# Order of the column maxima's parts on four engines in the cross-attention stage of a decoder layer

## The chip, the core and the metric

The kernel runs on one core of one Trainium2 chip. The metric is the device time of one execution in microseconds (us), the median of several runs. The engines are named as the profile names them: PE is the matrix engine (PEld its weight loads), DVE the vector engine, ACT the scalar engine, POOL the gpsimd engine and SP the engine that only issues DMAs here (its queue is SPq). Each engine runs its own instructions in program order and waits for semaphores that others raise.

## The reference, cut to what matters

One decoder layer on x of 16 items x 128 rows x 512 columns: attention, cross attention and a feed-forward network with rounded weights, each added to x. The change lies in the cross stage:

```
x = x + _L0_xattn_ref(_layernorm(x), ctx_2048, w_in, b_in, w_out, b_out, w_ct, b_ct, 64)

def _L0_xattn_ref(mask, encodings, ...):      # N=16 items, E=128, T=512, H=8 heads, d=16
    qkv = transpose(mask) @ w_in.T + b_in
    scores = einsum('bqhd,bkhd->bhqk', q, k) / sqrt(d)
    band = abs(idx[:, None] - idx[None, :]) <= local_size        # 64
    scores = where(band, scores, neg)
    attn = softmax(scores)
    o = einsum('bhqk,bkhd->bqhd', attn, v) @ w_out.T + b_out
    y = relu(transpose(o)) * encodings
    return einsum('nit,io->not', y, w_ct) + b_ct[None, :, None]
```

The feed-forward network that follows rounds its weights to -1, 0 and 1 after dividing by their mean size.

## The kernel before

The kernel has three stages, one after the other: attention, the cross stage (from about 627 to 1021 us of the profile) and the feed-forward stage. The cross stage is one function, `cross`. It is a hand-written pipeline over the 16 items: `steps` runs `step(b)` for b from -3 to 18 on each engine, and each step has eight slots (s = 0 to 7) of a pair of heads and half of the tiles each. Within a step PE works on three items: in each slot it computes scores of item b+1 for their maxima (`maximum_scores` into Sm), and scores of item b with the maxima already taken off (`shifted_scores` into Se); in slots 0 to 2 it also multiplies the exponentials of item b-1 with the values (`values`), and in later slots it projects item b+3.

**The maxima.** DVE reduces Sm into `mx` (L1292), and PE may write Sm of slot s only when `mx` of slot s-1 has been read. After four slots, half an item, PE turns the maxima (`maxima_turned`, L1054 and L1055, into bank Bb). They are then split into three bf16 parts: ACT copies the high part (`maxima_high`, L1136, tile x_m), DVE takes the remainder (`maxima_rest`, L1299, x_mr), POOL makes the middle and the low part (`maxima_low`, L1191 and L1193), and SP writes the three parts as three extra rows of the tile Q of that item (`maxima_rows`, L1249, three DMAs of 4 KB). With rows of ones in K beside them, `shifted_scores` subtracts the maxima inside the matmul. It waits for these rows (m_in) in slot 0 (half 0, slots 0 to 3) and slot 4 (half 1). Half 1 of item b is turned in slot 0 of step b, and is needed in slot 4 of the same step. Half 0 of item b+1 is turned in slot 4 of step b and needed in slot 0 of step b+1.

**The queue of SP.** q and k of an item are also kept as three bf16 parts (x_qp, x_kp): `keep` writes them to DRAM (q_parts, k_parts, 384 KB each) and `spread` reads them back in the layout that the matmuls want (tiles Q and K, 768 KB each, in three and four DMAs). `spread` waits until what `keep` wrote has landed. SP also loads the context of an item (x_ctxb, 256 KB, read by POOL in L1213) and one of the 12 pieces of the feed-forward weights (`load_piece`, L58 and L60, x_w_stage, up to 768 KB). Piece n is loaded at the end of step n-1; in slot 1 of step n DVE scales and rounds it (`offset`, L1316), ahead of the maxima of slot 2; ACT writes it out in slot 2 (L1181).

In a step of before, SP's order is: context of item b-2, spread q of b+2, keep k of b+2, rows of half 1 of b, spread k of b+2, rows of half 0 of b+1, keep q of b+3, piece b+1. The order of the other engines is in the code of `step`.

## Time and profile before

| | |
|---|---|
| median of 3 runs | 1240.86 us (1239.91 to 1244.84) |
| the profiled execution | 1235.82 us, its span 1234.0 us |
| PE, DVE busy, share of the span | 84%, 66% |
| ACT, POOL busy | 52%, 52% |
| TensorE clock granted, mean of the span | 0.945 of full speed |

The profile is one execution. Its page gives busy times and the costliest groups of instructions. Other views of the same execution are used below: a table of stretches of time, a list of who waited for whom, the instructions in order of time (the timeline; a bracket at the end of a row is the idle time of the engine just before the instruction, and what ended it), and the DMAs with their times from issue to landing. The times of a row count from the start of the span.

### The profile page before, as it was taken

The numbers are of one execution on the slowest core, as the hardware profiler recorded it, in microseconds if no ns is written. First come the engines' busy times: TensorE is split into PE (matmuls) and PEld (weight loads), VectorE is DVE, ScalarE is ACT, GpSimd is POOL, SyncE is SP. The second block draws the span as 40 slices with busy tenths as digits, with TensorE's granted clock in tenths as the row PEclk, the third lists the DMA queues.
The fourth block names the chain that finished last, engine by engine and source line by source line (L and its number), as shares of the span: only waits on it lengthen the run. The fifth ranks groups of instructions, "written<-read, shape, count | busy, mean of one in ns | idle before, by whom it ended". The sixth has DMA issues, their size and how long they took to land. (4 is left out here: it accounts for less than half of the span.)

```text
span 1234.0 us, 25423 instructions
## 1 busy us (share of the span) xinstructions
PE 1035.4 (84%) x9604; PEld 774.9 (63%) x9604; DVE 813.1 (66%) x1487; ACT 647.5 (52%) x1188; POOL 640.5 (52%) x584
## 2 busy tenths in 40 slices
PE   5689999999999999999635888989899954777675
PEld 5578887888888888887413666656566631333332
DVE  7678776666666666576334667676666645888884
ACT  5555545455454545556512566666556542455553
POOL 3665666566565657566315143434334334566653
PEclk9899999999999999999867899999999976899998
DMA  9043643233233332346336666665755200000000
GB/s 348 21 172 122 246 166 120 110 138 136 81 131 133 136 113 97 133 160 211 134 75 153 149 168 164 168 160 135 187 130 135 60 19 32 18 17 25 25 25 27
DMA packets 51135, 147.57 MB, mean 120 GB/s; under 512 B 10448, under 2 KB 24272, under 8 KB 39760
## 3 DMA queue, kind: packets, MB, share of 16 engines
q1 hardware_dynamic: 42288, 86.93, 25.3%
q0 software_dynamic: 8064, 58.72, 13.0%
q8 instruction: 75, 1.23, 0.4%
q10 hardware_dynamic: 672, 0.40, 0.1%
q14 instruction: 36, 0.29, 0.1%
HBM read 120.46 MB, written 25.17 MB: 118 GB/s over the span
## 5 line engine op out<-in xcount | busy, mean ns | idle before, releaser
L1292 DVE TENSOR_REDUCE mx<-Sm 128x4 f32<-128x768 f32 x128 | 122.4, 956 | 87.7 <-PE Sm L1032 87.2
L1130 ACT ACTIVATE x_ex<-Se 128x768 f32<-128x768 f32 x128 | 103.1, 805 | 116.4 <-PE Se L1032 116.0
L282 PE MATMUL Qb<-a_xTh,WqH 128*128 128x256 f32 x512 | 146.3, 286 | 3.1 <-DVE a_vl L800 3.0
L283 PE MATMUL Qb<-a_xTl,WqH 128*128 128x256 f32 x512 | 145.6, 284 | 0.0
L284 PE MATMUL Qb<-a_xTh,WqL 128*128 128x256 f32 x512 | 145.4, 284 | 0.0
L627 POOL TENSOR_TENSOR a_pr<-a_pr_plain,a_ph 128x512 fp32r<-128x512 f32 x64 | 83.6, 1307 | 110.2 <-ACT a_ph L447 110.0
L740 DVE TENSOR_TENSOR a_turned<-Qb,sinS 64x512 f32<-64x512 f32 (+1 forms) x144 | 94.9, 659 | 62.6 <-PE Qb L284 45.1
L609 POOL TENSOR_TENSOR a_ql<-a_rot,a_qh 128x512 fp32r<-128x512 f32 x64 | 83.9, 1315 | 98.4 <-ACT a_qh L467 98.2
L459 ACT ACTIVATE Lb<-Lb 128x512 f32<-128x512 f32 x64 | 37.2, 582 | 170.4 <-PE Ob L354 170.4
L367 PE MATMUL Yb<-a_WoH,a_oH 128*128 128x512 f32 x256 | 103.2, 403 | 5.5 <-POOL a_oN L605 5.5
L282 PEld LDWEIGHTS Qb<-a_xTh,WqH 128*128 128x128 f32 x512 | 98.6, 193 | 6.9 <-issue 2.4
L369 PE MATMUL Yb<-a_WoH,a_oN 128*128 128x512 f32 x256 | 101.3, 396 | 0.0
L368 PE MATMUL Yb<-a_WoL,a_oH 128*128 128x512 f32 x256 | 101.1, 395 | 0.0
L283 PEld LDWEIGHTS Qb<-a_xTl,WqH 128*128 128x128 f32 x512 | 98.6, 193 | 2.4
L284 PEld LDWEIGHTS Qb<-a_xTh,WqL 128*128 128x128 f32 x512 | 98.6, 193 | 0.0
L605 POOL TENSOR_TENSOR a_oN<-a_oN_plain,a_oH 128x512 fp32r<-128x512 f32 x64 | 84.9, 1327 | 3.0 <-ACT a_oH L439 3.0
L1024 PE MATMUL Sm<-band,ident_b 128*64 128x256 bf16 x512 | 54.9, 296 | 31.2 <-DVE mx L1292 18.2
L756 DVE TRANSPOSE_TENSOR_REDUCE a_rmax<-Sb 128x16 f32<-128x512 f32 x64 | 45.6, 712 | 51.6 <-PE Sb L334 51.5
L1024 PEld LDWEIGHTS Sm<-band,ident_b 128*64 128x64 bf16 x512 | 19.0, 111 | 90.3 <-issue 46.1
L636 POOL TENSOR_TENSOR Dg<-ident,a_negm 32x512 fp32r<-32x512 f32 x64 | 66.5, 1039 | 13.2 <-DVE a_negm L763 10.5
L1578 POOL TENSOR_TENSOR f_hg<-f_h,g 128x512 f32<-128x512 f32 (+1 forms) x48 | 56.0, 1181 | 32.3 <-DVE f_h L1658 32.3
L1482 PE MATMUL Gb<-gateQ,f_xqT 128*128 128x512 bf16 (+1 forms) x192 | 48.0, 374 | 29.1 <-DVE f_h L1658 27.4
(202 smaller groups left out, 2841.4 us busy)
## 6 DMA issues: line engine op xcount, KB each, us to landing
a_WoH<-wo_parts POOLq DMA_DIRECT2D x28, 1024.0 KB, 5.2
a_WoL<-wo_parts POOLq DMA_DIRECT2D x28, 1024.0 KB, 7.2
K<-k_parts SPq DMA_DIRECT2D x32, 256.0 KB, 4.8
q_parts<-x_qp SPq DMA_DIRECT2D x16, 384.0 KB, 3.0
Q<-q_parts SPq DMA_DIRECT2D x16, 384.0 KB, 5.6
k_parts<-x_kp SPq DMA_DIRECT2D x16, 384.0 KB, 7.4
a_w_stage<-in_gateT SPq DMA_DIRECT2D x8, 704.0 KB, 4.5
x_w_stage<-in_gateT SPq DMA_DIRECT2D x8, 704.0 KB, 5.1
```

What stands on the lines that cost most here:

```text
L282: pe.matmul(out, w_hi(k), xTh[:, k, :], start=(k == 0), stop=False)
L283: pe.matmul(out, w_hi(k), xTl[:, k, :], start=False, stop=False)
L284: mm = pe.matmul(out, w_lo(k), xTh[:, k, :], start=False, stop=(k == KD - 1))
L367: pe.matmul(Yb[s % 2][:, :], high, WoH[u % 2][:, i, :], start=(i == 0), stop=False)
L368: pe.matmul(Yb[s % 2][:, :], high, WoL[u % 2][:, i, :], start=False, stop=False)
L369: mm = pe.matmul(Yb[s % 2][:, :], low, WoH[u % 2][:, i, :], start=False, stop=(i == HG - 1))
L605: pool.tensor_tensor(oL[:, s % 2, :], oN[:, s % 2, :], oH[:, s % 2, :].bitcast(F32), ALU.subtract).then_inc(oL_ready, 1)
L609: pool.tensor_tensor(rot_dst(False, True, par, r), rbuf(par, r)[:, 0:rot_width(r)], rot_dst(True, False, par, r).bitcast(F32), ALU.subtrac ...
L627: pool.tensor_tensor(pl[:, :], pr[:, :], ph[:, :].bitcast(F32), ALU.subtract).then_inc(pl_ready, 1)
L740: dve.tensor_tensor(dst[to:to + hi - lo, 0:width].rearrange("p (j c) -> p j c", c=P), bank[lo:hi, 0:width].rearrange("p (j c) -> p j c", c=P),
L1130: act.activation(ex[:, (PAIRS * b + p) % RING, 4 * hf * WIN:4 * (hf + 1) * WIN].rearrange("p (j c) -> p j c", j=2), Se[:, :, 0:2 * WIN], A ...
L1292: dve.tensor_reduce(mx[:, half, at:at + 4].rearrange("p (j a) -> p j a", j=2), Sm[:, :, 0:2 * WIN].rearrange("p j (a c) -> p j a c", a=2), ...
```

## The change

No instruction is added or removed in the cross stage; several stand in another place of their engine's program. For half 1 of item b, the high part moves on ACT from slot 1 to slot 0 (ahead of the exponentials of slot 0), the remainder on DVE from slot 1 to slot 0 (ahead of the update of X), the low parts on POOL ahead of the low part of k, and the rows on SP to the front of the step. For half 0 of item b+1, high part and remainder move from slot 5 to slot 4. On SP keep k now stands ahead of spread q, and the load of the context moves from the front of the next step to the end of this one, ahead of the weight piece; it loads the same item into the same place.

```
--- before.py
+++ after.py
@@ -1146,7 +1146,7 @@
 
             def step(b):
                 for s in range(SLOTS):
-                    if s == 1 and real(b):
+                    if s == 0 and real(b):
                         maxima_high(b, 1)
                     if s == 3 and real(b - 1):
                         wait(act, pv_full, b)
@@ -1156,7 +1156,7 @@
                         wait(act, out_full, b - 1)
                         wait(act, wct_full, b - 2)
                         act.activation(gate[:, :], Bb[:, :], ACT.Relu, bias=t["bo"][:, 0:1]).then_inc(gate_ready, 1)
-                    if s == 5 and real(b + 1):
+                    if s == 4 and real(b + 1):
                         maxima_high(b + 1, 0)
                     if s == 6 and real(b + 3):
                         high(qp, 0, b + 3, q_full, q_kept, q_high)
@@ -1197,6 +1197,8 @@
                 pool.tensor_tensor(dst[:, 2, :], rest[:, :], dst[:, 1, :], ALU.subtract).then_inc(ready, 1)
 
             def step(b):
+                if real(b):
+                    maxima_low(b, 1)
                 if real(b + 2):
                     low(kp, kr, b + 2, k_mid, k_low)
                 if b == -1:
@@ -1205,8 +1207,6 @@
                         wait(pool, k_ones, i)
                         pool.memset(K[i][ROWS:SHIFTED, :, :], 1.0).then_inc(k_ones, 1)
                     wait(pool, k_ones, len(K))
-                if real(b):
-                    maxima_low(b, 1)
                 if real(b - 2):
                     wait(pool, gate_ready, b - 1)
                     wait(pool, ctx_in, 16 * (b - 1))
@@ -1249,20 +1249,19 @@
                     sp.dma_start(to, m3[half][:, k, :]).then_inc(m_in[half], 16)
 
             def step(b):
-                if real(b - 2):
-                    wait(sp, y_ready, b - 2)
-                    sp.dma_start(ctxb[:, :], dram["ctx"][b - 2]).then_inc(ctx_in, 16)
-                if real(b + 2):
-                    spread("q", Q, Q_RUNS, b + 2, q_kept, q_in)
-                    keep("k", kp, b + 2, k_low, k_in, K_IN, k_kept)
                 if real(b):
                     maxima_rows(b, 1)
                 if real(b + 2):
+                    keep("k", kp, b + 2, k_low, k_in, K_IN, k_kept)
+                    spread("q", Q, Q_RUNS, b + 2, q_kept, q_in)
                     spread("k", K, K_RUNS, b + 2, k_kept, k_in)
                 if real(b + 1):
                     maxima_rows(b + 1, 0)
                 if real(b + 3):
                     keep("q", qp, b + 3, q_low, q_in, Q_IN, q_kept)
+                if real(b - 1):
+                    wait(sp, y_ready, b - 1)
+                    sp.dma_start(ctxb[:, :], dram["ctx"][b - 1]).then_inc(ctx_in, 16)
                 if 0 <= b + 1 < len(PIECES):
                     wait(sp, w_whole, b)
                     load_piece(sp, dram, b + 1, w_stage[(b + 1) % 2]).then_inc(w_in[(b + 1) % 2], 16)
@@ -1334,12 +1333,12 @@
                     if real(b + 1):
                         maxima(b + 1, s)
                     if s == 0:
+                        if real(b):
+                            maxima_rest(b, 1)
                         if real(b - 3):
                             wait(dve, wct_full, b - 2)
                             dve.scalar_tensor_tensor(out=t["X"][:, b - 3, :], in0=Ab[:, :], scalar=t["bct"][:, 0:1], in1=t["X"][:, b - 3, :],
                                                      op0=ALU.add, op1=ALU.add).then_inc(x_new, 1)
-                    if s == 1 and real(b):
-                        maxima_rest(b, 1)
                     if s == 3 and real(b - 1):
                         wait(dve, o_ready, b)
                         wait(dve, oU_scaled, b - 1)
@@ -1347,12 +1346,12 @@
                             ins = dve.stream_shuffle(rl[:, hh, :], oU[:, hh, :], [XD * (1 - hh) + i % XD for i in range(32)])
                         ins.then_inc(sums_ready, 1)
                     if s == 4 and real(b + 1):
+                        maxima_rest(b + 1, 0)
                         if real(b + 3):
                             normalised(b + 3)
                         head_values(b + 1, 0)
                     if s == 5 and real(b + 1):
                         head_values(b + 1, 1)
-                        maxima_rest(b + 1, 0)
                     if s == 6 and real(b + 3):
                         rest(qp, qr, 0, b + 3, q_high, q_low, q_rest)
                     if s == 7 and real(b + 3):
```

The queue of SP in a step with a weight piece, from the rows of half 0 to spread k of the next step. Names in the rows: x_m the parts of the maxima, x_qp and x_kp the parts of q and k in SBUF, q_parts and k_parts the same in DRAM, x_w_stage the weight piece, x_ctxb the context. Before:

```order
L1249 DMA Q<-x_m 1x32x64 [waits x_m_low]
L1249 DMA Q<-x_m 1x32x64 x2
L1234 DMA q_parts<-x_qp 128x3x512 [waits x_q_low,x_q_in]
L58 DMA x_w_stage<-in_gateT 128x1408 [waits x_w_whole]
L1254 DMA x_ctxb<-in_ctx 128x512 [waits x_y_ready]
L1241 DMA Q<-q_parts 48x4096 [waits x_se_full,x_q_kept]
L1241 DMA Q<-q_parts 32x4096
L1241 DMA Q<-q_parts 16x4096
L1234 DMA k_parts<-x_kp 128x3x512 [waits x_k_low,x_k_in]
L1249 DMA Q<-x_m 1x32x64 [waits x_m_low]
L1249 DMA Q<-x_m 1x32x64 x2
L1241 DMA K<-k_parts 16x4096 [waits x_se_full,x_k_kept]
```

The same place now:

```order
L1249 DMA Q<-x_m 1x32x64 [waits x_m_low]
L1249 DMA Q<-x_m 1x32x64 x2
L1234 DMA q_parts<-x_qp 128x3x512 [waits x_q_low,x_q_in]
L1264 DMA x_ctxb<-in_ctx 128x512 [waits x_y_ready]
L58 DMA x_w_stage<-in_gateT 128x1408 [waits x_w_whole]
L1249 DMA Q<-x_m 1x32x64 [waits x_m_low]
L1249 DMA Q<-x_m 1x32x64 x2
L1234 DMA k_parts<-x_kp 128x3x512 [waits x_k_low,x_k_in]
L1241 DMA Q<-q_parts 48x4096 [waits x_se_full,x_q_kept]
L1241 DMA Q<-q_parts 32x4096
L1241 DMA Q<-q_parts 16x4096
L1241 DMA K<-k_parts 16x4096 [waits x_se_full,x_k_kept]
```

The second group of rows of the maxima moved from behind spread q and keep k to just behind the weight piece, keep k moved ahead of spread q, and the context ahead of the piece.

On ACT, from the end of one step to slot 2 of the next, before:

```order
L1145 ACTIVATE x_qp<-x_qr 128x512 [waits x_q_rest]
L1130 ACTIVATE x_ex<-Se 128x768 [waits x_se_full] x2
L1145 ACTIVATE x_kp<-x_kr 128x512 [waits x_k_rest]
L1136 ACTIVATE x_m<-Bb 32x64 [waits x_m_in1,x_t_full]
L1130 ACTIVATE x_ex<-Se 128x768 [waits x_se_full] x2
```

The same place now:

```order
L1145 ACTIVATE x_qp<-x_qr 128x512 [waits x_q_rest]
L1130 ACTIVATE x_ex<-Se 128x768 [waits x_se_full]
L1136 ACTIVATE x_m<-Bb 32x64 [waits x_m_in1,x_t_full]
L1130 ACTIVATE x_ex<-Se 128x768 [waits x_se_full]
L1145 ACTIVATE x_kp<-x_kr 128x512 [waits x_k_rest]
L1130 ACTIVATE x_ex<-Se 128x768 [waits x_se_full] x2
```

The high part (L1136) moved from behind the exponentials of slot 0 and the middle part of k to ahead of both.

## Rows read from the trace of the kernel before

**Rows 1.** Table of stretches, two steps: PE, PEld, DVE, ACT, POOL busy, PEclk, DMA.
```profile
827.13:847.00 19.87, 18.68 (x348) 12.96 (x345) 14.85 (x25) 13.40 (x20) 8.36 (x9) 1.00 0.66 164
847.00:872.37 25.37, 20.76 (x347) 13.66 (x345) 14.63 (x25) 13.98 (x21) 8.36 (x9) 0.93 0.64 157
```

**Rows 2.** Who waited for whom, PE, 676 to 976 us: total us, times, longest.
```profile
PE Sm L1024 <- DVE mx L1292: 12.1, 8, 3.5
PE Se L1024 <- DMA Q<-x_m: 10.2, 10, 2.1
```

**Rows 3.** Timeline of PE around slots 4 and 5: start us, duration us.
```profile
811.08 0.41 PE L1024 MATMUL Se<-band,ident_b 128*64 128x256 bf16 x4 [0.18 <-ACT x_ex L1130]
...
830.09 0.41 PE L1024 MATMUL Se<-band,ident_b 128*64 128x256 bf16 x4 [0.81 <-DMA Q<-x_m]
...
831.71 0.41 PE L1024 MATMUL Se<-band,ident_b 128*64 128x256 bf16 x4 [0.38 <-ACT x_ex L1130]
```

**Rows 4.** Timeline of all engines, one step: how the rows of half 1 come about.
```profile
817.71 0.39 SPq L1234 DMA_DIRECT2D q_parts<-x_qp  x1
817.99 0.96 DVE L1292 TENSOR_REDUCE mx<-Sm 128x4 f32<-128x768 f32 x1 [0.61 <-PE Sm L1032]
818.01 0.28 PE L1055 MATMUL Bb<-ident,mx 128*32 128x64 f32 x2
818.14 0.49 SPq L58 DMA_DIRECT2D x_w_stage<-in_gateT  x1
818.67 0.59 SPq L1254 DMA_DIRECT2D x_ctxb<-in_ctx  x1
...
820.20 0.20 ACT L1136 ACTIVATE x_m<-Bb 32x64 bf16<-32x64 f32 x1
...
821.52 0.20 DVE L1299 TENSOR_TENSOR x_mr<-Bb,x_m 32x64 f32<-32x64 f32 x1
...
822.19 0.30 POOL L1193 TENSOR_TENSOR x_m<-x_mr,x_m 32x64 bf16<-32x64 f32 x1
...
823.46 1.80 SPq L1249 DMA_DIRECT2D Q<-x_m  x3
```

**Rows 5.** L1316, all twelve (ns min/median/max, first and last start); timelines, pieces 6 and 7.
```profile
L1316 DVE TENSOR_SCALAR x_w_stage<-x_w_stage,w_inv x12: 753/953/1020, 678.4 to 910.7; 128x1408 f32<-128x1408 f32 x8, 128x1536 f32<-128x1536 f32 x3, 128x1024 f32<-128x1024 f32 x1
...
804.29 0.95 DVE L1316 TENSOR_SCALAR x_w_stage<-x_w_stage,w_inv 128x1408 f32<-128x1408 f32 x1 [3.66 <-DMA x_w_stage<-in_gateT]
...
806.16 0.41 PE L1024 MATMUL Sm<-band,ident_b 128*64 128x256 bf16 x4 [2.06 <-DVE mx L1292]
...
822.73 0.95 DVE L1316 TENSOR_SCALAR x_w_stage<-x_w_stage,w_inv 128x1408 f32<-128x1408 f32 x1 [1.01 <-DMA x_w_stage<-in_gateT]
...
825.96 0.41 PE L1024 MATMUL Sm<-band,ident_b 128*64 128x256 bf16 x4
```

**Rows 6.** DMAs, us to landing: piece 7, keep q, piece 9; last, all of L1249.
```profile
x_w_stage<-in_gateT SPq DMA_DIRECT2D x1, 704.0 KB, 4.6
...
q_parts<-x_qp SPq DMA_DIRECT2D x1, 384.0 KB, 2.9
...
x_w_stage<-in_downT SPq DMA_DIRECT2D x1, 768.0 KB, 7.8
...
DMA to landing us min/median/max: 1.6/2.5/7.2
```

**Rows 7.** The start of the cross stage, timelines of SP, POOL and PE.
```profile
636.98 1.33 POOL L1197 TENSOR_TENSOR x_kp<-x_kr,x_kp 128x512 bf16<-128x512 f32 x1
...
640.90 0.42 SPq L1234 DMA_DIRECT2D k_parts<-x_kp  x1
...
646.97 1.69 SPq L1241 DMA_DIRECT2D K<-k_parts  x4
...
653.34 0.64 PE L1024 MATMUL Sm<-band,ident_b 128*64 128x256 bf16 x4 [12.76 <-DMA K<-k_parts]
```

**Rows 8.** DMA busy tenths, 636 to 654 us in 40 slices of 0.45 us.
```profile
DMA  0000699000989949499599500086999699939950
```

More of the change, by code:

```diff
@@ L1148, in step @@
                 for s in range(SLOTS):
-                    if s == 1 and real(b):
+                    if s == 0 and real(b):
                         maxima_high(b, 1)
@@ L1158, in step @@
                         act.activation(gate[:, :], Bb[:, :], ACT.Relu, bias=t["bo"][:, 0:1]).then_inc(gate_ready, 1)
-                    if s == 5 and real(b + 1):
+                    if s == 4 and real(b + 1):
                         maxima_high(b + 1, 0)
@@ L1199, in step @@
             def step(b):
+                if real(b):
+                    maxima_low(b, 1)
                 if real(b + 2):
@@ L1207, in step @@
                     wait(pool, k_ones, len(K))
-                if real(b):
-                    maxima_low(b, 1)
                 if real(b - 2):
@@ L1251, in step @@
             def step(b):
-                if real(b - 2):
-                    wait(sp, y_ready, b - 2)
-                    sp.dma_start(ctxb[:, :], dram["ctx"][b - 2]).then_inc(ctx_in, 16)
-                if real(b + 2):
-                    spread("q", Q, Q_RUNS, b + 2, q_kept, q_in)
-                    keep("k", kp, b + 2, k_low, k_in, K_IN, k_kept)
                 if real(b):
@@ L1260, in step @@
                 if real(b + 2):
+                    keep("k", kp, b + 2, k_low, k_in, K_IN, k_kept)
+                    spread("q", Q, Q_RUNS, b + 2, q_kept, q_in)
                     spread("k", K, K_RUNS, b + 2, k_kept, k_in)
@@ L1265, in step @@
                     keep("q", qp, b + 3, q_low, q_in, Q_IN, q_kept)
+                if real(b - 1):
+                    wait(sp, y_ready, b - 1)
+                    sp.dma_start(ctxb[:, :], dram["ctx"][b - 1]).then_inc(ctx_in, 16)
                 if 0 <= b + 1 < len(PIECES):
@@ L1336, in step @@
                     if s == 0:
+                        if real(b):
+                            maxima_rest(b, 1)
                         if real(b - 3):
@@ L1340, in step @@
                                                      op0=ALU.add, op1=ALU.add).then_inc(x_new, 1)
-                    if s == 1 and real(b):
-                        maxima_rest(b, 1)
                     if s == 3 and real(b - 1):
@@ L1349, in step @@
                     if s == 4 and real(b + 1):
+                        maxima_rest(b + 1, 0)
                         if real(b + 3):
@@ L1354, in step @@
                         head_values(b + 1, 1)
-                        maxima_rest(b + 1, 0)
                     if s == 6 and real(b + 3):
```

## The prediction

> **What bounds the kernel now.** I read the stage first in the table of stretches. Cut at the projection to v in slot 3 (L1105), a step takes 19 to 25 us, and PE is busy for 18.68 us of the 19.87 in a quiet one [rows 1]. DVE has 14.85, ACT 13.40, POOL 8.36. So PE is the bound of the stage, and only what makes PE wait costs time. The list of PE's waits from 676 to 976 us has two large entries that this change can touch [rows 2]. First, 10.2 us in 10 waits, up to 2.1 us each, of the shifted scores for the extra rows of the maxima (DMA Q<-x_m). In the timeline all ten stand in slot 4, where half 1 is needed [rows 3]. Second, 12.1 us in 8 waits for the maxima of DVE; six of them, 10.8 us, stand in slot 3 and follow a wait of DVE for a weight piece (pieces 0, 1, 2, 6, 9, 10: 3.5, 0.7, 0.8, 2.1, 1.5, 2.3), the other two, of 0.6, stand in the first steps.
>
> The path to the rows is in the timeline of one step [rows 4]. PE has turned the maxima by 818.29 (818.01 + 0.28). ACT copies the high part only at 820.20, DVE takes the remainder only at 821.52, POOL is done at 822.49, and SP issues the rows at 823.46, behind spread q and keep k. PE has to stop for them, from 829.28 to 830.09 [rows 3]. Hardly any of this path is work; it is places in queues.
>
> **Part 1: high part, remainder, low parts, rows to the front.** The new path, from the same rows: ACT starts at 818.3 and takes 0.20; DVE is free at 818.95 (817.99 + 0.96) and takes 0.20; POOL is through 0.77 after DVE's end (822.49 less 821.72); so the parts are ready near 819.9, and SP, through with its last issue at 819.26, sends the rows at about 820.0 instead of 823.46. That is 3.5 us earlier, and behind 704 KB of weights instead of behind weights, 768 KB of q and 384 KB of k. A row that was issued alone lands in 1.6 us, the worst took 7.2 [rows 6]. Even 7.2 gives 827.2, under the 829.28 at which PE wants them. The ten waits go: **-10.2 us**. What is late next there is ACT. The wait for the exponentials that follows each longer wait is 0.38, and where there was no wait for rows it is 0.18 [rows 3]. Eight of the ten had such a follower: 8 x 0.2 = **-1.6 us**.
>
> What the moves delay, all of it at nothing: on ACT 0.20 us ahead of the exponentials of slot 0, whose scores PE computes only after the turning that ACT waits for; on DVE 0.20 ahead of the update of X, whose reader is slots away; on POOL the low part of k, which waits for ACT's middle part, now behind the maxima's. In slot 4 DVE takes the remainder ahead of the copies of the values, in a dense stretch, with the maxima of slot 5 behind them. PE has no wait for mx in slots 4 to 7 of the full steps (the eight of [rows 2] stand in slot 3 or in the first two), so 0.2 should be hidden. If that cover is gone, it costs 0.2 x 12 = 2.4 us. On the other side ACT loses 0.1 us between the logarithm and the exponential of the sums, which releases POOL, keep q and the weight piece: each piece may start 0.1 earlier.
>
> **Part 2: the context goes ahead of the weight piece.** Before, the piece was issued at 818.14 and the context behind it [rows 4]; now 256 KB stand before it. Where each piece lands decides the maxima of slot 2 and with them PE in slot 3: piece 6 reached DVE at 804.29, and PE started slot 3 at 806.16, 1.87 later, after 2.06 of waiting. Piece 7 reached it at 822.73, so PE could have started at 824.60, and came at 825.96: 1.36 of slack [rows 5]. The same reading of the 12 executions of L1316, 678.4 to 910.7, against PE's slot 3 gives the slack of the ten pieces that have a context ahead now (2 to 11): five had none and made PE wait or just not (2, 6, 8, 9, 10), piece 5 0.04, 4 0.62, 7 1.36, 3 1.98, 11 4.9.
>
> The delay itself isn't in the trace. Keep q and piece 7 together, 1088 KB, went from the issue at 817.71 to 822.73, 5.02 us. Taking off the 1.6 of a tiny DMA [rows 6], that is 3.4 us or 320 KB per us; 256 KB are 0.8 us. Bounds: 0, if the two travel beside each other at no loss, and 1.4, if the issue of 0.59 comes on top (it should be hidden, since keep q, issued at 817.71, landed 2.9 later [rows 6]). I take 0.8, as the queue was full at that time, less the 0.1 of part 1: 0.7. Cost: pieces 2, 6, 8, 9, 10 5 x 0.7, piece 5 0.66, piece 4 0.08: **+4.2 us**. At 0 it is nothing; at 1.4 it is 5 x 1.4 + 1.36 + 0.78 + 0.04 = 9.2.
>
> That one waits for the other is what the Trainium skill says (DMA: Bandwidth & Descriptors, section Queues, rings and completion order): descriptors of one ring are consumed in order, and the semaphore's increment lands after every earlier write of its engine. By that rule the bound of 0 falls, and with it the sum of -14.5 us which would go with it; by the trace alone it stands.
>
> **Part 3: keep k ahead of spread q.** In the full steps keep k stays where it was in time (three issues come before it either way, of spread q or of the rows), spread q is sent 1 to 2 us later, but its tile is needed only in the next step, and spread k, which waits for k_parts, comes earlier: nothing. But at the start of the stage PE waits 12.76 us for the first K, the longest wait of all [rows 7]. There POOL had the low part of k ready at 638.31 (636.98 + 1.33), and SP issued keep k at 640.90, behind spread q; K was read back from 646.97, and PE began at 653.34. Now keep k can go at 638.35, while nothing else is being moved. The DMA row shows two gaps of three slices, 1.35 us each: one before spread q, one before spread k [rows 8]. The first is now filled by most of keep k, the second closes, since k_parts has landed while spread q still runs: 2 x 1.35 = **-2.7 us**. Bounds: 0, if the bytes take longer together, and -5.5, if K is read back 5.5 us earlier (638.35 + 2.9 as for keep q = 641.3, and spread k behind spread q) and lands so much earlier.
>
> **The clock.** In the step of 847 us the granted clock is 0.93, one short spell at 1.2 instead of 2.4 GHz, and PE is busy for 20.76 instead of 18.68 us [rows 1]: 2 us. It followed the longest wait for rows. Waits of about 2 us and more seem to bring this on. That wait goes (-2.0), but the wait of piece 6 grows from 2.06 to 2.8 (+2.0 if it brings such a spell). I leave both out.
>
> **Sum.** -10.2 - 1.6 + 4.2 - 2.7 = -10.3 us. From the profiled 1235.82 that is 1225.5. The profiled execution is 5 us below the median of the runs shown, 1240.86; against the median the forecast is **1230.5 us**, -0.8%. Its own range is 1226 to 1234.5.
>
> **Rivals.** (a) *The context costs its full 1.4 us, and the start gives nothing.* -11.8 + 9.2 = -2.6: 1238. For it: the queue is busy 0.64 to 0.66 of each step [rows 1]; against it: the gaps of rows 8. Chance 0.16.
>
> (b) *Pieces land late all over.* Piece 7 landed after 4.6 us, but piece 9 after 7.8 [rows 6] (6 and 10 nearly as late): one laggard among the engines that move it. With the context ahead the piece is open to such a delay for longer. If all land after 7.5 plus 0.7, then, slack taken off, pieces 2 to 10 cost 17.3 us instead of 4.2, and with waits of 2.2 to 3.5 us in six steps six spells of low clock, 12 us more: -14.5 + 17.3 + 12 = +14.8, 1256. It decides from a mean extra delay of about 2.1 us per piece, where the cost of part 2 passes 14.5. Chance 0.07; this is the case on the slower side.
>
> (c) *The late pieces get on time.* The laggards had spread q's large blocks beside them, right behind the context; now these come after the rows and keep k, 1 to 2 us later. If pieces 6, 9 and 10 land like the others, most of their waits (1.5 to 2.3 each) and their share of part 2 go: 6.9 less, 1223.6. Chance 0.13.
>
> (d) *The clock takes part of it.* Two more waits pass the length that brought a spell (pieces 6 and 9 at 2.8 and 2.2): +4.0, 1234.5 to 1236. Chance 0.14.
>
> (e) *The rows land no earlier.* They stand behind the piece in a queue that moves in order. Then only the start gains and part 2 is paid: -2.7 + 4.2 = +1.5, 1242.4. Against it the 7.2 us of the worst landing. Chance 0.04.
>
> **Chances.** Forecast 0.46, (a) 0.16, (b) 0.07, (c) 0.13, (d) 0.14, (e) 0.04. A measurement of this kernel can tell about 0.5%, 6.2 us, from no change. Faster by more: the forecast's cases but for the edge, (c), and a little of (d): 0.60. Within 0.5%: 0.33. Slower: (b), 0.07. The range of 1222 to 1240 leaves out (b), (e) and the ends of (a).
>
> **What would show it.** Right: no wait of Se for DMA Q<-x_m in the list of PE's waits; rows of half 1 issued about 2.3 us after keep q instead of 5.8; the first K no longer the end of a wait of 12.8 but of about 10 us; L1316 0.7 us later after keep q (5.7 instead of 5.0 in the step of piece 7); PE's waits for mx up from 12.1 to about 16. Wrong: landings of pieces of 7 us and more in most steps (b), steps with a granted clock under 1.00 behind a wait of slot 3 (d), or a new entry in PE's list, such as scores of slots 5 or 6 behind the copies of the values. If the rows are early and the time doesn't move, the context's place is the cause.

## The result and the profile after

| | before | after |
|---|---|---|
| median, first comparison | 1240.38 us (1237.95 to 1244.84) | 1221.12 us (1220.54 to 1221.54) |
| ratio, with its 95% interval | | 0.984 [0.9812, 0.9869] |
| median, another chip | 1235.96 us (1231.91 to 1248.14) | 1221.45 us (1218.13 to 1226.01) |
| ratio | | 0.9873 [0.9801, 0.9945] |
| profiled execution | 1235.82 us | 1220.54 us |

The change makes the kernel 1.6% faster, 19.3 us between the medians, and 1.3%, 14.5 us, in the second comparison; both intervals lie under 1. The direction is the forecast's; the size is nearly twice the -10.3 us of the sum in the first comparison (1.4 times in the second), and the time lies just under the range of 1222 to 1240.

Where it was gained is read best in one long stretch of each profile: the fifteen steps from the first projection to v to the last. The table of stretches gives their length, PE busy (with the number of instructions), PEclk, DMA share and GB/s. First the kernel before:

```profile
661.33:976.41 315.08, 280.87 (x4972) 0.96 0.62 149
```

The kernel after, the same fifteen steps, and below them three single steps, to be held against [rows 1]:

```profile
660.67:960.68 300.01, 275.61 (x4973) 0.98 0.68 156
...
721.23:743.30 22.07, 20.11 (x349) 0.92 0.70 160
...
824.25:844.08 19.83, 18.78 (x348) 1.00 0.75 174
...
904.84:923.75 18.91, 18.72 (x349) 1.00 0.58 126
```

The stretch is 15.1 us shorter, practically all of the 15.3 us between the two profiled executions. Two things are in it. PE stands still less, and PE is busy 5.3 us less (280.87 less 275.61) for the same work: its clock is granted in full more of the time. Steps with a piece now take 20 to 21 us (one 22.1); the ones without (the last row) 18.9.

What PE waited for from 676 to 976 us of the kernel after, with total, times and longest; it answers [rows 2]:

```profile
PE Sm L1024 <- DVE mx L1291: 18.8, 17, 2.9
PE XY L1075 <- issue: 0.7, 1, 0.7
PE Se L1024 <- ACT x_ex L1130: 0.4, 1, 0.4
```

The wait for the rows (DMA Q<-x_m) is gone, and so are nearly all waits for the exponentials. The wait for the maxima has grown; in the fifteen steps it went from 14.3 to 20.5 us. In slots 4 and 5, where [rows 3] show a stop of 0.81 and one of 0.38, PE's rows carry no bracket now (timeline of after):

```profile
826.32 0.41 PE L1024 MATMUL Se<-band,ident_b 128*64 128x256 bf16 x4
...
827.94 0.41 PE L1024 MATMUL Se<-band,ident_b 128*64 128x256 bf16 x4
```

Timelines of after, one step, the answer to [rows 4] and to the second half of [rows 5]:

```profile
814.09 0.39 SPq L1234 DMA_DIRECT2D q_parts<-x_qp  x1
...
814.47 0.28 PE L1055 MATMUL Bb<-ident,mx 128*32 128x64 f32 x2
814.52 0.48 SPq L1264 DMA_DIRECT2D x_ctxb<-in_ctx  x1
814.78 0.21 ACT L1136 ACTIVATE x_m<-Bb 32x64 bf16<-32x64 f32 x1 [1.23 <-PE Bb L1055]
815.05 0.58 SPq L58 DMA_DIRECT2D x_w_stage<-in_gateT  x1
...
816.00 0.30 POOL L1193 TENSOR_TENSOR x_m<-x_mr,x_m 32x64 bf16<-32x64 f32 x1
816.32 2.54 SPq L1249 DMA_DIRECT2D Q<-x_m  x3
...
821.21 0.95 DVE L1315 TENSOR_SCALAR x_w_stage<-x_w_stage,w_inv 128x1408 f32<-128x1408 f32 x1 [3.14 <-DMA x_w_stage<-in_gateT]
...
823.08 0.41 PE L1024 MATMUL Sm<-band,ident_b 128*64 128x256 bf16 x4 [1.42 <-DVE mx L1291]
```

High part, remainder and low parts now follow the turning at once, and the rows are issued 1.6 us after it (816.32 less 814.75) instead of 5.2. The price is in the last two rows: DVE gets the piece 7.1 us after keep q, not 5.0 as in [rows 5], and PE waits 1.42 us where it had 1.36 us in hand.

The start of the stage, against [rows 7]:

```profile
640.38 0.37 SPq L1234 DMA_DIRECT2D k_parts<-x_kp  x1
...
643.04 1.78 SPq L1241 DMA_DIRECT2D K<-k_parts  x4
...
652.68 0.64 PE L1024 MATMUL Sm<-band,ident_b 128*64 128x256 bf16 x4 [9.91 <-DMA K<-k_parts]
```

### The profile page after: what moved, and what is told of

Its sections match the earlier page's. It is cut to its first block and busy times, and to the rows that moved or that the text cites. A ratio compares the mean times of both kernels' runs of the same rounds, so it can differ in the third digit from the quotient of the medians.

```text
span 1218.7 us, 25407 instructions
## 1 busy us (share of the span) xinstructions
PE 1030.6 (85%) x9588; PEld 776.0 (64%) x9604; DVE 812.1 (67%) x1487; ACT 652.0 (53%) x1188; POOL 644.8 (53%) x584
## 5 line engine op out<-in xcount | busy, mean ns | idle before, releaser
L1024 PE MATMUL Sm<-band,ident_b 128*64 128x256 bf16 x512 | 54.2, 293 | 35.6 <-DVE mx L1291 24.5
L1213 POOL TENSOR_TENSOR x_gate<-x_gate,x_ctxb 128x512 f32<-128x512 f32 x16 | 20.3, 1269 | 113.2 <-ACT x_gate L1158 113.2
L1024 PEld LDWEIGHTS Sm<-band,ident_b 128*64 128x64 bf16 x512 | 18.5, 110 | 95.2 <-DVE mx L1291 58.0
L636 POOL TENSOR_TENSOR Dg<-ident,a_negm 32x512 fp32r<-32x512 f32 x64 | 66.6, 1041 | 13.4 <-DVE a_negm L763 10.5
```

## The experiments

Diffs are against the kernel after unless "before" is named; they show the lines of SP's `step` that move. The columns of the table are, for each kernel's profiled execution, the fifteen steps as above: their length, PE busy in them, and the waits of PE in them for the rows (Q<-x_m), for the maxima (mx), for K (K<-k_parts), for the exponentials, and for "issue".

| kernel | steps | PE busy | rows | mx | K | exp. | issue |
|---|---|---|---|---|---|---|---|
| before | 315.1 | 280.9 | 10.2 | 14.3 | | 4.3 | 4.5 |
| before, again | 314.0 | 279.6 | 6.5 | 16.0 | | 5.2 | 5.9 |
| after | 300.0 | 275.6 | | 20.5 | | 0.4 | 0.7 |
| after, again | 299.1 | 274.6 | | 17.5 | | 0.4 | 3.7 |
| e1, part 2 undone | 294.5 | 275.2 | | 11.7 | | | 4.6 |
| e3, part 1 alone | 298.8 | 277.0 | | 12.4 | 2.2 | | 4.1 |
| e2, part 3 alone | 350.0 | 296.7 | 37.5 | 8.9 | | 2.9 | 3.6 |
| e6, engines alone | 317.2 | 282.1 | 10.6 | 13.9 | | 4.1 | 5.4 |
| e7, queue alone | 345.2 | 293.5 | 0.5 | 6.0 | 38.8 | 0.3 | 3.4 |
| e4, piece behind spread k | 289.8 | 273.5 | 4.7 | 5.9 | 1.7 | | 0.9 |
| e8, piece behind the rows | 285.4 | 273.4 | | 5.9 | 2.1 | | 1.2 |
| e11, e8 and part 2 undone | 283.7 | 271.9 | | 5.3 | 2.7 | | 0.9 |
| e10, before, piece moved | 320.6 | 286.8 | 22.5 | 5.6 | | 4.3 | 0.8 |

### Part 2 undone (e1)

```
@@ step(b), SP
+                if real(b - 2):
+                    wait(sp, y_ready, b - 2)
+                    sp.dma_start(ctxb[:, :], dram["ctx"][b - 2]).then_inc(ctx_in, 16)
                 if real(b):
                     maxima_rows(b, 1)
...
-                if real(b - 1):
-                    wait(sp, y_ready, b - 1)
-                    sp.dma_start(ctxb[:, :], dram["ctx"][b - 1]).then_inc(ctx_in, 16)
```

> The changed kernel with its part 2 undone: the context is loaded at the front of the next step again, behind the weight piece. If the context delays each piece as the prediction says, DVE reaches the piece 0.7 us sooner after keep q, PE's waits for mx fall by about 4 us, and the time is 4.2 us under the changed kernel: 1217. Rival: the context's place costs nothing, since what decides is the slowest of the engines that move the piece; then the time is 1221 within 1, or above it if late pieces (7 us and more) come back.

Measured: 1214.48 us (1209.53 to 1217.68), ratio to before 0.9798 [0.9746, 0.985]. Waits of PE, 676 to 976 us:

```profile
PE Sm L1024 <- DVE mx L1291: 9.9, 12, 3.2
```

The intervals of this and of the kernel after overlap, so the times alone do not separate them; the waits for the maxima do, 18.8 us against 9.9. From keep q to DVE's reading of the piece, over pieces 2 to 10, it takes 5.83 us on average here and 6.95 in the kernel after: the context ahead costs each piece 1.1 us. PE's waits behind those nine pieces add up to 2.8 us here and to 11.9 after (8.6 in the second profile of after). In the fifteen steps mx falls by 8.8 us, of which 3.9 come back as waits for issue; the steps are 5.5 us shorter.

### Part 1 alone (e3)

```
@@ e1, and in step(b), SP
                 if real(b + 2):
-                    keep("k", kp, b + 2, k_low, k_in, K_IN, k_kept)
                     spread("q", Q, Q_RUNS, b + 2, q_kept, q_in)
+                    keep("k", kp, b + 2, k_low, k_in, K_IN, k_kept)
                     spread("k", K, K_RUNS, b + 2, k_kept, k_in)
```

> The changed kernel with parts 2 and 3 undone, that is part 1 alone: high part, remainder, low parts and rows at the front, context and keep k in their old order. The prediction's part: -11.8, 1228.6, with pieces 6, 9 and 10 still late and spells of low clock behind them. Rival: the waits for the rows were what made the spells of low clock and the waits for instructions; then part 1 alone brings most of the whole gain, 1224 or less.

Measured: 1218.77 us (1218.61 to 1222.95), 0.9829 [0.9788, 0.987]. The first K is waited for as long as before (timeline of e3):

```profile
655.18 0.64 PE L1024 MATMUL Sm<-band,ident_b 128*64 128x256 bf16 x4 [11.79 <-DMA K<-k_parts]
```

So part 1 carries the gain: 1.7% of the before, some 20 us, where the sum gave it 11.8. Part 3, which is what e1 has more than this, is 4.3 us by the medians of the same chip; the intervals of the two overlap, so the times alone don't show it.

### Part 3 alone (e2)

```
@@ before, step(b), SP
                 if real(b + 2):
-                    spread("q", Q, Q_RUNS, b + 2, q_kept, q_in)
                     keep("k", kp, b + 2, k_low, k_in, K_IN, k_kept)
+                    spread("q", Q, Q_RUNS, b + 2, q_kept, q_in)
```

> The kernel before with part 3 alone: keep k ahead of spread q, all else as before. The prediction's part: the first K ends a wait of 10 instead of 12.8 us, -2.7, and the ten waits for the rows stay: 1237.7. Rival: the gain of the change that the prediction did not have (5 to 9 us) comes from the later spread q, which leaves the weight piece alone in the queue; then pieces 6, 9 and 10 land in about 5 us here too, the waits for mx fall by 5 us or more, and the time is 1232 or less.

Measured: 1270.82 us (1260.0 to 1274.46), 1.0233 [1.0163, 1.0303]. A miss, by over 30 us. Waits of PE, 676 to 976 us, SP's timeline and PE's:

```profile
PE Se L1024 <- DMA Q<-x_m: 35.0, 13, 3.8
```

```profile
815.01 1.43 SPq L1241 DMA_DIRECT2D Q<-q_parts  x3
816.48 1.78 SPq L1249 DMA_DIRECT2D Q<-x_m  x3
...
824.58 0.41 PE L1024 MATMUL Se<-band,ident_b 128*64 128x256 bf16 x4 [2.80 <-DMA Q<-x_m]
```

What makes the rows late is their issue, not the trip. Keep k now stands at the head of the step and waits for POOL's low part of k (28.5 us in 12 waits of SP from 676 to 976 us, none before); spread q and the rows stand behind it. On average over the fifteen steps the rows of half 1 are issued 5.9 us after the turning, instead of 4.7, and the last of the three lands 7.1 us after the first issue, instead of 6.9. "In full steps nothing", the prediction's word on part 3, holds only where the rows have gone ahead.

How little it takes is seen from when PE is there. In the fourteen steps from the second on, the time from the turning to the last landing, and to PE's arrival at slot 4, is on average 11.9 and 11.6 us before, 13.4 and 10.7 in e2, and 7.0 and 11.3 after. Before, the rows and PE come at the same time.

### The two halves of part 1 (e6, e7)

e6 has the order of ACT, DVE and POOL of the kernel after and SP's queue of the kernel before. e7 has the engines of before, and on SP this:

```
@@ before, step(b), SP
+                if real(b):
+                    maxima_rows(b, 1)
                 if real(b + 2):
                     spread("q", Q, Q_RUNS, b + 2, q_kept, q_in)
                     keep("k", kp, b + 2, k_low, k_in, K_IN, k_kept)
-                if real(b):
-                    maxima_rows(b, 1)
                 if real(b + 2):
                     spread("k", K, K_RUNS, b + 2, k_kept, k_in)
```

> The changed kernel with SP's queue put back as before: only ACT, DVE and POOL have their instructions moved, and the rows of half 1 stand behind spread q and keep k. If it is the place in the queue that counts, the rows are sent 1 us sooner and still land behind 1.1 MB: most of the waits for rows stay, 1234 to 1238. Rival: the chain on the engines is what counts; then the waits go and the time is that of part 1, 1219 to 1223.

Measured: 1235.33 us (1232.85 to 1243.79), 0.9973 [0.9945, 1.0001].

```profile
PE Se L1024 <- DMA Q<-x_m: 10.6, 8, 2.6
```

The wait for the rows stays (10.6 against 10.2 in [rows 2]): parts that are ready early gain little while the rows stand behind q and k on SP: these are issued 4.6 us after the turning here, 4.7 before.

> The kernel before with one change: SP sends the rows of half 1 at the front of the step, ahead of spread q and keep k; ACT, DVE and POOL stay. The rows are then ready at 822.5 of the step of the profile and leave at once, 1 us sooner than before, but with no 768 and 384 KB ahead of them; spread q and keep k wait for them, 2 us later than before. If the bytes ahead of the rows are what made PE wait, the ten waits go and the time is 1219 to 1228. Rival: what waits behind the rows becomes late instead, K of the next item first (its wait was up to 0.7 us with part 1 alone), and the time is 1232 or more.

Measured: 1264.95 us (1263.1 to 1266.71), 1.0193 [1.0153, 1.0234]. Waits and a step's timelines:

```profile
PE Sm L1024 <- DMA K<-k_parts: 38.8, 13, 4.4
```

```profile
810.73 0.28 PE L1055 MATMUL Bb<-ident,mx 128*32 128x64 f32 x2
...
815.55 0.30 POOL L1193 TENSOR_TENSOR x_m<-x_mr,x_m 32x64 bf16<-32x64 f32 x1
...
815.88 2.71 SPq L1249 DMA_DIRECT2D Q<-x_m  x3
818.70 1.44 SPq L1241 DMA_DIRECT2D Q<-q_parts  x3
820.23 0.38 SPq L1234 DMA_DIRECT2D k_parts<-x_kp  x1
826.12 1.69 SPq L1241 DMA_DIRECT2D K<-k_parts  x4
...
832.35 0.41 PE L1024 MATMUL Sm<-band,ident_b 128*64 128x256 bf16 x4 [3.26 <-DMA K<-k_parts]
```

SP stands at the rows until their parts are done, 4.9 us after the turning, and all behind them comes later by that. Spread q is issued 7.7 us after the turning and keep k 9.2; in the kernel before these are 2.4 and 3.7, as its timeline has them, against a turning that ends at 818.29 [rows 4]:

```profile
820.65 1.25 SPq L1241 DMA_DIRECT2D Q<-q_parts  x3
822.00 1.42 SPq L1234 DMA_DIRECT2D k_parts<-x_kp  x1
```

Spread k can't go until keep k has landed, and PE waits for K in 13 steps. The rows themselves are no longer waited for (0.5 us). So neither half of part 1 brings its share: -0.3% and +1.9%, together -1.7%.

### What is left in slot 3: the place of the piece (e4, e8, e11, e10)

In e4 the piece goes right behind spread k, ahead of the rows of half 0. In e8 it goes behind these:

```
@@ step(b), SP
                 if real(b + 1):
                     maxima_rows(b + 1, 0)
+                if 0 <= b + 1 < len(PIECES):
+                    wait(sp, w_whole, b)
+                    load_piece(sp, dram, b + 1, w_stage[(b + 1) % 2]).then_inc(w_in[(b + 1) % 2], 16)
                 if real(b + 3):
                     keep("q", qp, b + 3, q_low, q_in, Q_IN, q_kept)
...
-                if 0 <= b + 1 < len(PIECES):
-                    wait(sp, w_whole, b)
-                    load_piece(sp, dram, b + 1, w_stage[(b + 1) % 2]).then_inc(w_in[(b + 1) % 2], 16)
```

> The changed kernel with the weight piece of the next step issued right behind spread k, some 10 us sooner, instead of last in the step. If the waits of DVE for the piece are what is left of PE's waits in the full steps (about 16 of 18 us for mx), they go and the time is 1221 - 15 = 1206. Rival: what is moved out of the way there comes back as waits for the rows of half 0, or for q of the next item, which now stand behind the piece; then 1212 to 1221.

Measured: 1209.63 us (1205.17 to 1212.4), 0.9749 [0.97, 0.9797].

```profile
PE Se L1024 <- DMA Q<-x_m: 4.7, 6, 1.2
PE Sm L1024 <- DVE mx L1291: 4.1, 7, 1.0
```

The waits for the maxima fall from 18.8 to 4.1 us, but now the rows of half 0 stand behind 704 KB and are late in six steps.

> The changed kernel with the weight piece issued behind the rows of half 0, where SP stands idle for 4 us, instead of behind keep q and the context. In the run with the piece behind spread k the rows of half 0 had to wait for it (4.7 us in 6 waits). Here nothing should wait for piece or rows: 4 us under that run, 1205. Rival: the piece is then in the way of keep q, spread q and K of the next item, and the time is 1210 or more.

Measured: 1203.32 us (1201.94 to 1206.54), 0.9698 [0.966, 0.9735]. Waits, and SP's timeline of a step:

```profile
PE Sm L1024 <- DVE mx L1291: 4.1, 7, 1.0
```

```profile
798.00 1.78 SPq L1249 DMA_DIRECT2D Q<-x_m  x3
799.83 0.58 SPq L58 DMA_DIRECT2D x_w_stage<-in_gateT  x1
804.29 0.38 SPq L1234 DMA_DIRECT2D q_parts<-x_qp  x1
```

The piece is issued 4.5 us ahead of keep q, in a time when SP had nothing else to issue. Most steps with a piece take 18.9 us, as those without one do in the kernel after. This version beats both kernels: 3.0% under before, and its interval lies wholly under that of the kernel after.

> The best version so far (changed kernel, piece behind the rows of half 0, 1203.3) with the context back at the front of the next step. The context's place matters only through the piece behind it; with the piece away from there the time stays within 1.5 us of 1203. Rival: the context in front of the rows and of keep k delays these, and the time is 1206 or more.

Measured: 1202.69 us (1200.88 to 1203.72), 0.9715 [0.9649, 0.9781], the same as e8. In neither is the context ahead of the piece, and its place then costs nothing that can be measured: part 2's price is what the context does to the piece behind it.

> The kernel before with one change: the weight piece is issued behind the rows of half 0 instead of behind keep q; chain, rows and keep k stay where they were. If 704 KB of weights in one queue with everything else are what made rows and maxima late, waits for rows and mx both go and the time falls by 20 us or more, 1219 or less, without the change. Rival: the rows still stand behind 768 and 384 KB of q and k and their chain of places is the cause; then only the waits for mx in slot 3 go (7 us in the steps after the first) and most of the waits for rows stay: 1230 or more.

e10 is the kernel before with this move of the piece alone. Measured: 1240.3 us (1231.86 to 1244.92), 1.0011 [0.9975, 1.0047].

```profile
PE Se L1024 <- DMA Q<-x_m: 22.5, 12, 4.3
...
PE Sm L1024 <- DVE mx L1292: 3.3, 4, 1.8
```

Waits for the maxima fall from 12.1 to 3.3 us, and those for the rows grow from 10.2 to 22.5. What is worth 18 us behind the change is worth nothing ahead of it. The rows aren't later: from the turning to their last landing it takes 11.9 us on average, as before. It is PE that is sooner, at slot 4 after 10.3 us instead of 11.6, since it no longer stops for the maxima in slot 3. So the stops for the pieces had covered for the rows, and only where the rows come earlier is it worth taking them away. A second thing cancels in the queue: keep q, now behind the piece, lands later, and SP's wait for it ahead of spread q grows from 19.9 to 42.1 us (676 to 976 us); the rows are issued 1.1 us later for it, and land 1.1 us sooner after their issue.

### Both kernels again (e5, e9)

> The kernel before, unchanged, for a second profiled execution beside the one that the prediction was made from (1235.8, while the median is 1239 to 1241). If the first was a typical one, this one has the same kinds of waits on PE within 1 or 2 us each and the miss lies in the terms. Rival: executions of before differ in how late the pieces and rows land, and a slower one (1239 or more) shows some us more of waits for rows and mx and more spells of low clock, all of which the change removes: then part of the miss is that the sum was made from a lucky execution.

> The changed kernel, unchanged, beside the next two on one chip, for a second profiled execution and a time to set the run with the context behind the piece against (1214.5, ratio 0.980). If part 2 costs what the waits of those two traces say (PE's waits in the full steps 5 us apart), this one is at 0.984 of the kernel before, 1220. Rival: the two ratios differed only by chip, and this one is at 0.980 or less.

Measured: 1239.54 us in a single execution for before, and 1221.45 us, 0.9873 [0.9801, 0.9945], for after, so its rival (0.980 or less) is not borne out; the fifteen steps 314.0 and 299.1 us. The difference of the steps repeats to 0.2 us (14.9 against 15.1); the split among the waits does not: mx 17.5 instead of 20.5, issue 3.7 instead of 0.7, rows 6.5 instead of 10.2.

The second profile of before is 3.7 us longer than the first, but its fifteen steps are 1.1 us shorter. What is longer lies outside them: they begin 3.8 us later (665.10 instead of 661.33), and what follows them takes 1.0 us more. PE comes to its wait for the first K at 640.59 in the first and at 645.00 in the second, and anywhere between 640.5 and 645.0 us in the fourteen profiles, though none of the edits touches the attention stage. So the execution that the prediction was made from was a fast one in a part that the change leaves alone.

### Does a busier PE keep its clock? (e12)

e12 is e7 with work for PE while it waits for K: from the second item on, at slot 0 and once the maxima of the slot ahead are read, PE runs the four mask matmuls into Sm ten times over. They write the values that the real ones then write again, so nothing of the result changes.

```
@@ e7, maximum_scores(b, s), PE
+                if s == 0 and b > 0:
+                    wait(pe, mx_ready, SLOTS * b)
+                    for n in range(10):
...
+                                pe.matmul(at, t["ident_b"][:, TS * hh:TS * hh + TS], masks, start=True, stop=True, skip_group_check=True)
                 if s == 0:
                     wait(pe, q_in, Q_IN * (b + 1))
                     wait(pe, k_in, K_IN * (b + 1))
```

> The run in which only SP's queue was changed (1265: 13 waits for K of 2.6 to 4.4 us in slot 0, a spell of 1.2 GHz behind nearly each), with PE kept busy in those waits: from item 1 on, ten extra sets of the four band matmuls, 2.4 us in all, are written into Sm ahead of the wait for K and then overwritten by the same values. No byte comes sooner and no chain is shorter. If the spells of low clock are brought on by the waits and cost what the busy time says (18 us over the steps), they go and the time falls by 10 to 17 us, to 1248 to 1255. Rival: the spells come from something else in those steps, or cost nothing beyond the wait; then the time stays at 1265 or rises by what the extra matmuls overrun.

Measured: 1257.85 us (1254.02 to 1259.14), 1.0155 [1.011, 1.0199], against e7's 1264.95 and 1.0193 [1.0153, 1.0234]. The fifteen steps, first of e7, then of e12:

```profile
661.23:1006.38 345.15, 293.53 (x4972) 0.92 0.56 136
```

```profile
662.28:997.32 335.04, 311.60 (x5573) 0.98 0.59 140
```

One filling, and the real work behind it:

```profile
828.40 2.37 PE L1045 MATMUL Sm<-band,ident_b 128*64 128x256 bf16 x40
...
831.57 0.41 PE L1024 MATMUL Sm<-band,ident_b 128*64 128x256 bf16 x4 [0.80 <-issue]
```

Fifteen fillings of 2.37 us are 35.6 us of PE. Taken off 311.60 this leaves 276.0 for the work of the kernel, which took 293.53 in e7: 17.5 us less, and the stretch is 10.1 us shorter though PE does more. The ratios' intervals overlap, so the whole kernel's gain of 7 us is likely and not shown; the granted clock of the stretch, 0.92 to 0.98, is plain: thirteen of the fifteen steps of e7 are under 1.00, and in e12 the first three. The gain came out under what I expected (1248 to 1255 us); 11.4 us of waits called issue, behind the fillings, stand where the waits for K were, and whether they are the same waits is open.

## What of the prediction held, and why it came out too small

The direction came as forecast, and the waits that were to go went. The size did not: 1221.1 us was measured where 1230.5 was forecast, under the range of 1222 to 1240. The step that failed is the one on the clock. The prediction held one spell removed against one that might come back ("-2.0", "+2.0") and left both out; what the profiles show in its place is 5.3 us less of PE busy for the same instructions, about as much as the whole gap between the sum's -10.3 and the -15.3 us of the two profiles. The other terms that were off cancel to 0.3. The other 4 us, up to the medians, come from setting the sum of one profile against a median.

**Part 1, the rows: right.** The sum took away the ten waits, -10.2 us. They are gone in after, e1 and e3. (Nine of the ten stood in slot 4, for half 1; the one at 694.82, of 0.38 us, stood in slot 0, for half 0.) The rows were to be issued 2.3 us after keep q; it is 2.23 (816.32 less 814.09), against 5.75 in [rows 4]. Issuing is only part of the trip; the landings of L1249, least, median and worst, were the worry of rival (e), and the trace of after says, against [rows 6]:

```profile
DMA to landing us min/median/max: 1.7/3.1/5.0
```

Rival (e) is out. What the section did not say is that both halves are needed at once. It costed the engines' moves at nothing and the queue's as the gain, where e7 shows the queue's move alone at +1.9%: the parts are done 1.6 us after the turning instead of 4.2 [rows 4], and that is what makes room for a wait at the front of SP's queue.

**The exponentials: right in kind, too small.** -1.6 us, from 0.2 for each of eight stops, which took the 0.18 of the quiet steps as what would stay. The list went from 4.3 to 0.4 us in the fifteen steps: -3.9. Without stops for rows nothing of it stays.

**Part 2, the context: the size of the delay too small, the sum near.** The delay was taken as 0.7 us between 0 and 1.4; against e1 it is 1.1. The prediction's own mark, 5.7 us from keep q in the step of piece 7, reads 7.1. The Trainium skill (DMA: Bandwidth & Descriptors, section Queues, rings and completion order) says that descriptors of one ring are consumed in order and that the increment of the semaphore lands after the earlier writes of its engine; the 1.1 us agree, and the bound of 0 is out. The slack that the reading gave to pieces 3, 4, 5 and 7 is gone too: all nine pieces of 2 to 10 have PE wait (seven of the nine in the second profile of after). It went with the context and not because PE, not stopped by the rows, comes to slot 3 sooner; in e1, where it isn't stopped either, these four have 1.5, 0.4, 0.4 and 2.0 us in hand. Against this stands what rival (c) foresaw. From keep q to DVE the late pieces 6, 9 and 10 took 7.8, 8.2 and 7.9 us before, 7.0, 6.6 and 7.5 after, and 6.5, 5.9 and 6.7 in e1. The landings of all twelve pieces in the trace of after, least, median and worst:

```profile
DMA to landing us min/median/max: 4.8/5.8/6.5
```

No piece takes 7 us and more now ([rows 6] have 7.8), so rival (b) is out. The two errors nearly cancel: the waits for the maxima grew by 6.2 us, 4.2 were forecast. The lone 3.8 us that the waits for issue fell (4.5 to 0.7) were in no term; they were 3.7 in the second profile of after and 4.1 and 4.6 in e3 and e1. What brings them can be narrowed down. They stand where no semaphore is waited for, mostly inside the multiplication with the values (L1075), and in the same steps of different executions (the longest, 2.3 and 2.4 us, in the twelfth step of both profiles of before). The profile also has the DMAs that fetch instructions (queue q8, 16 KB each, one in some 6 us). Of the 24 such stops of 0.6 us and more in the fifteen steps of all profiles but e12's, 21 end 1.3 to 1.8 us after such a fetch has ended. So PE seems to wait there for its instructions, which come over the same DMA engines; e4, e8, e10 and e11, with the piece moved, have none as long. No run here tests it by itself.

**Part 3: right at the start, wrong as a statement on full steps.** PE's first scores come 0.66 us earlier (653.34 to 652.68) in a stage where POOL has the low part of k 2.04 us later (640.35 for 638.31), so 2.7 us as forecast, and the wait fell from 12.76 to 9.91. The first wait for K is 9.95 and 9.56 us in e1 and e2, which have keep k ahead, and 11.8 in e3, which hasn't. The first wait itself is within 0.2 us of the "about 10" that was to show it. Both bounds (0 and -5.5) are out: spread k was issued 2.7 us after keep k instead of 6.1, but its bytes then shared the queue with spread q. The full steps are e2's lesson: by itself the order costs 30 us.

**The clock: the term left out.** "-2.0 +2.0" should have been about -5 us. For the same instructions PE was busy 280.87 us before and 275.61 after, 271.92 in e11, where the clock of the stretch is 1.00. So low clock cost some 9 us of the steps before and 3.7 after. From the second on, four of the fifteen steps before had a granted clock under 1.00 (0.92, 0.93, 0.86, 0.91), and two after (0.92 and 0.92). The four spells of 1.2 GHz that the kernel before has in its full steps, by the table of stretches (PE busy, PEclk, DMA):

```profile
852.90:856.50 3.60, 3.60 (x22) 0.53 0.78 143
893.90:897.40 3.50, 3.50 (x24) 0.51 0.36 83
914.40:917.80 3.40, 3.38 (x14) 0.51 0.54 140
962.20:965.60 3.40, 3.40 (x44) 0.50 0.57 119
```

The first follows the wait for the rows that the prediction named, 2.14 us at 851.28. The others follow these:

```profile
892.64 0.41 PE L1024 MATMUL Sm<-band,ident_b 128*64 128x256 bf16 x4 [2.28 <-DVE mx L1292]
914.42 0.58 PE L1075 MATMUL XY<-x_ex,Vw 64*32 64x128 f32 x2 [2.32 <-issue]
960.11 0.41 PE L1024 MATMUL Se<-band,ident_b 128*64 128x256 bf16 x4 [1.39 <-DMA Q<-x_m]
```

So two of the four stood behind waits for the rows, one of only 1.39 us, one behind piece 10 and one behind a wait for issue. In the kernel after all four are gone and one has come, behind the 1.61 us at 720.06. (The 0.92 of the second step, behind the wait for piece 0, is in both.) The 2.0 that were added rested on piece 6, whose wait was to grow to 2.8 us; it fell to 1.35, and before, at 2.06, it had brought no spell. "Waits of about 2 us and more" was no rule. The prediction asked for one spell and not for the other three. Rival (d), the clock taking part of the gain, is out with the opposite sign. The gain in clock repeats, the stops behind it do not: in the second pair of profiles PE is busy 5.0 us less (279.6 and 274.6), and the spells that went stood at stops of 2.42 us for piece 10 and 2.37 for issue, none at one for the rows. That stops bring on the low clock was an argument in the prediction; e12 bears it out, with the waits filled and the clock back. Which share of the 5.3 us is owed to the rows isn't shown.

**The sum.** In the fifteen steps: waits -11.7 (33.3 to 21.6), PE busy -5.3, small stops that the list leaves out +1.9: -15.1. The start gives -2.7, the attention stage, which the change doesn't touch, +2.0, the end +0.5: -15.3, from 1235.82 to 1220.54. The 5 us that are missing against -10.3 are the size of the clock's term; the other misses (exponentials -2.3, maxima +2.0, issue -3.8, small stops +1.9, attention and end +2.5) cancel to 0.3. The other 4 us, up to the 19.3 of the medians, come from the step that set the profile's sum against the median: the profiled execution of before lay 5 us under its median, that of after on it. In the second pair of profiles the difference is 18.5 us (1239.54 and 1221.05). Of the 3.2 us that it is more than in the first pair, 2.7 come from where the fifteen steps begin, 3.4 us apart instead of 0.7, and none from the steps: the attention stage again. The kernel before ranges over 1231.9 to 1248.1 us in its 44 executions, the one after over 1218.1 to 1226.0 in 8; whether one of them varies more can't be said from so few.

## What to carry to other kernels

A wait put first in the queue of an in-order issuer is good only when the work it waits for has been moved up as well: look at both halves together, and ask of each half alone what stands behind it. When a large load shares a queue with small urgent ones, send it right behind the small ones, in the stretch in which the issuer has nothing else to do, not in the order in which its buffer happens to come free; here that was worth as much again as the change, once the rows were early, and nothing before. Ask of a stop that you take away what it was giving time to: in e10 the next wait took it all. And count the low clock as a price of all stops of the bound engine together: compare its busy time for the same instructions, not the one spell next to the one stop.

## What the runs showed of the hardware

- Spells of lower clock (1.2 instead of 2.4 GHz) followed stops of PE of 1.4 to 4.4 us in steps of about 20 us: in e7, with a stop of up to 4.4 us in nearly every step, the granted clock of the steps was 0.92, and the same work took 293.5 us of PE instead of 272 to 276. But not every such stop did it: after a wait of 1.61 us the step of 721.23 has 0.92, after one of 1.86 the step of 884.84 us has 1.00.
- DMAs of 4 KB in SP's queue land after 1.6 to 7.4 us (the worst in e6), by what is ahead of them. From the issue of the first of three to the landing of the last it takes 6.9 us on average behind weights, context, q and k (before), 5.1 behind context and weights (after), and 3.7 where the piece is sent ahead of keep q (e8). What stands ahead in the queue is not free for the small ones behind.
- PE stopped for up to 2.4 us in the middle of a run of matmuls where it waited for no semaphore, in most cases 1.3 to 1.8 us after a 16 KB instruction fetch had ended.
- The issue of the same three small DMAs took SP 1.78 us at 798.00 in e8 and 2.54 at 816.32 in after, where 256 and 704 KB had just been issued ahead; what makes issuing slower wasn't tried.
- The order of the same DMAs costs some 2.6% here: with the engines' order of before, 1270.8 us in e2 against 1238.9; with that of after, 1235.3 in e6 against 1202.7 in e11.
